# Decoder of two post-LN layers on one core: other orders of the stages on all queues, other banks for most fills, waits of the start-up at their first use

## The reference

```
x = norm(x + L0_attn(x))        # 16 heads; q, k, v lifted to a latent of 32; rotary embedding on
                                # q and k; causal softmax; latent back to 16; output projection
x = norm(x + L0_xattn(ctx, x))  # linear attention: q @ (k^T v), k and v from ctx, no softmax
x = norm(x + L0_ffn(x))         # fp4(x) @ fp4(w_gate), fp4(w_up), 704 wide; silu(g)*u; fp4; w_down
x = norm(x + L1_attn(x))        # causal softmax attention with v = x, plus a moving-average part:
                                #   e = x[1:] - y[:-1];  qa = -leaky(-q*s);  ka = sigmoid(k2*s*0.02)
                                #   y_ma = tril(qa @ ka^T) @ e
x = norm(x + L1_xattn(x, ctx, mask))  # softmax attention over ctx, output projection
x = norm(x + relu(x @ W1 + b1) @ W2 + b2)      # 1024 wide
x = norm(x + fp6(x) @ fp6(w) + b)              # one quantized linear layer
```

## Time and profile before

| | us |
|---|---|
| median of 3 runs | 916.19 (915.95 to 919.12) |
| profiled execution | 917.46 |
| its span, from first to last instruction | 915.5 |
| PE busy | 832.2 (91%) |
| PE weight loads | 667.2 (73%) |
| DVE busy | 709.4 (77%) |
| ACT busy | 635.8 (69%) |
| POOL busy | 301.5 (33%) |
| mean granted clock of TensorE | 0.968 |

### The profile page before, as it was taken

The page is one execution under the profiler, slowest core; times in us unless marked ns, Lnnn a source line. Parts: engine busy times, 40 slices in busy tenths (PEclk is TensorE's granted clock), DMA queues, the critical chain, the costliest instruction groups (busy, mean ns, idle before and its releaser), DMA issues.

```text
span 915.5 us, 29466 instructions
## 1 busy us (share of the span) xinstructions
PE 832.2 (91%) x11901; PEld 667.2 (73%) x11910; DVE 709.4 (77%) x1619; ACT 635.8 (69%) x2507; POOL 301.5 (33%) x554
## 2 busy tenths in 40 slices
PE   5877799999999999999999999999999999998873
PEld 4655677878778787878787787878787876876752
DVE  6996686878787978888787879788787878777552
ACT  3525578696959687786969686877869686866641
POOL 1232213233332434342333334342423334323221
PEclk9888799999999999999999999999999999999977
DMA  9300300000101000000001000000001000000000
GB/s 336 145 1 12 99 19 8 3 25 2 34 2 31 8 27 6 13 20 8 28 1 34 9 28 9 23 15 8 20 8 29 10 7 14 7 3 10 10 2 11
DMA packets 24440, 24.87 MB, mean 27 GB/s; under 512 B 2304, under 2 KB 22640, under 8 KB 24176
## 3 DMA queue, kind: packets, MB, share of 16 engines
q1 hardware_dynamic: 24304, 22.98, 7.7%
HBM read 18.80 MB, written 2.10 MB: 23 GB/s over the span
## 4 chain that ended last, share of the span: by engine, by line
PE 69%; ACT 17%; DVE 8%; POOL 2%; issue 2%; DMA 1%; SPq 0%; DVEq 0%; POOLq 0%; ACTq 0%
PE bank L1416 39%; PE s_tile L1416 21%; ACT prob L897 9%; PE bank L1537 3%; PE bank L1627 3%; ACT k_ L930 2%; ACT probT L836 1%; POOL rstd L762 1%; ACT x_ L945 1%; DVE stats L1127 1%; DVE y_ L1142 1%; ACT cross_ L921 1%; PE bank L1657 1%; DVE rope_ L1181 1%; ACT q_ L973 1%
## 5 line engine op out<-in xcount | busy, mean ns | idle before, releaser
L897 ACT ACTIVATE prob<-s_tile,low 128x128 f32<-128x128 f32 x768 | 273.4, 405 | 14.2 <-DVE low L1189 14.2
L897 ACT ACTIVATION_READ_ACCUMULATOR prob<-s_tile,low 128x1 f32 x768 | 188.1, 245 | 0.0
L1189 DVE TENSOR_REDUCE low<-s_tile 128x4 f32<-128x512 f32 x192 | 121.2, 680 | 31.0 <-PE s_tile L1416 30.9
L760 POOL TENSOR_TENSOR var_eps<-mean_var,rsq 128x1 f32<-128x1 f32 x144 | 31.1, 216 | 263.3 <-DVE mean_var L1129 263.1
L836 ACT ACTIVATE probT<-bank 128x512 f32<-128x512 f32 x180 | 94.1, 618 | 26.3 <-PE bank L1627 26.3
L762 POOL TENSOR_TENSOR rstd<-var_eps,rsq 128x1 f32<-128x1 f32 x144 | 86.7, 602 | 11.3
L836 ACT ACTIVATE xt_<-bank 128x256 f32<-128x256 f32 x66 | 25.4, 385 | 90.6 <-PE bank L1537 90.3
L1627 PE MATMUL bank<-cst,prob 32*128 32x32 f32 x2880 | 62.5, 225 | 17.9 <-ACT prob L897 14.9
L1627 PEld LDWEIGHTS bank<-cst,prob 32*128 32x128 f32 x2880 | 54.6, 139 | 31.1 <-ACT prob L897 18.1
L799 POOL TENSOR_TENSOR k_<-q_,q_scale 128x256 f32<-128x256 f32 x32 | 19.8, 618 | 164.4 <-DVE q_ L1088 164.4
L1416 PE MATMUL bank<-w_gu,xt_ 128*128 128x352 f32 x232 | 71.8, 460 | 0.7 <-ACT xt_ L836 0.7
(11 more groups left out here) (263 smaller groups left out, 1983.0 us busy)
## 6 DMA issues: line engine op xcount, KB each, us to landing
xtin<-in_xT SPq DMA_DIRECT2D x16, 128.0 KB, 2.4
next_<-in_x SPq DMA_DIRECT2D x16, 128.0 KB, 6.8
ct_<-in_ctxT SPq DMA_DIRECT2D x16, 128.0 KB, 7.5
w<-in_w SPq DMA_DIRECT2D x2, 1024.0 KB, 10.7
out<-x_ SPq DMA_DIRECT2D x16, 128.0 KB, 1.7
next_<-x_ SPq DMA_DIRECT2D x16, 127.0 KB
rowt<-in_rows SPq DMA_DIRECT2D x1, 1664.0 KB, 9.0
w<-in_gate_up SPq DMA_DIRECT2D x2, 512.0 KB, 6.0
```

Of the source, the lines that this page charges most:

```text
L760: pool.tensor_tensor(var_eps[:, b:b + 1], mean_var[:, b, 1:2], rsq[:, 0:1], ALU.add) .then_inc(eps_in, 1)
L897: ins = act.activation(prob[:, r, c * P:(c + 1) * P], bank[r][:, c * P:(c + 1) * P], ACT.Exp, bias=low[:, b, at0:at0 + 1], accum_out=sums[ ...
L1189: dve.tensor_reduce(low[:, b, 4 * r:4 * r + 4], rows4(src[:, :]), AX_X, ALU.max, negate=True)\
```

## The change

It changes the three tables, and moves the two blocks of waits to the stages that need them first. No stage is added or removed, and no stage's own instructions change.

*Orders.* Of PE's 918 steps 310 keep their place, the others move by 1.8 places on average, 45 at most. DVE's 736 move by 2.9 on average, nearly all of it in `x1_mask`, which goes 64 to 75 places earlier; ACT's 709 by 1.6 (241 stay, 24 at most), POOL's 304 by 1.3, SP's 73 by 3.0 (11 at most). The moves differ from tile to tile. Places before and after:

| engine, step (tile) | before | after |
|---|---|---|
| PE `l0_project` (0), `v_bias` | 3, 2 | 0, 1 |
| PE `l0_lat` (0), `l0_v` (0), `l0_v` (1) | 5, 6, 15 | 2, 3, 4 |
| PE `warm2`, `warm0`, `turn_up0` | 0, 1, 4 | 9, 22, 7 |
| PE `turn_up1`, `turn_up2` | 20, 21 | 23, 29 |
| PE `l0_scores` (0), `x0_kv` (2), `l0_project` (3) | 10, 35, 63 | 8, 43, 83 |
| PE `warm5`, `warm11`, `warm4`, `warm6` | 782, 813, 832, 901 | 775, 841, 877, 882 |
| PE `l0_mix0` (15), `l0_spread` (15) | 803, 814 | 784, 807 |
| DVE `l0_rope` (0), `quant_up1`, `quant_up2` | 5, 4, 7 | 4, 6, 13 |
| ACT `l0_norm` (8), `l1_project` (7), `l1_ka` (7) | 333, 334, 335 | 335, 333, 334 |
| SP `l0_project` (6) | 22 | 28 |

The banks of nearly all fills outside `s_tile` change, and where one bank served tiles 5 to 13 before, it now differs from tile to tile; the masks of `COVERED` follow (1,326 bits before, 1,368 after). The diff cut to lines of each kind:

```diff
-    "l0_mix0.t0": '4455644444444446', "l0_mix0.t1": '6567455555555554', "l0_mix0.t2": '3324766666666665',
+    "l0_mix0.t0": '7656567267312553', "l0_mix0.t1": '4507441054225640', "l0_mix0.t2": '6775312622677161',
...
-    "l1_project.qk2": '5712222222222227', "l1_project.k": '7030000000000051', "p_warm2": 4,
+    "l1_project.k": '3632231424320023', "l1_project.qk2": '4521016031743366', "p_warm2": 5,
...
-    ("f0_up", "f0_turn_x.xt"): 0x0002, ("f0_up", "free.s0"): 0xbff2, ("f0_up", "free.s1"): 0x7fff,
...
+    ("f0_up", "free.s0"): 0x6842, ("f0_up", "free.s1"): 0xe055, ("f0_up2", "f0_turn_x.xt"): 0xffff,
...
-            act.wait_ge(came["cols"], 16)
-            act.wait_ge(set_up, SETUP_STEPS.index("x1q_mb1") + 1)
-            act.wait_ge(cleared, 4)
+            def made(i, b, name):
+
+                if i + b == 0:
+                    act.wait_ge(set_up, SETUP_STEPS.index(name) + 1)
...
             def l1_project(i, b):
+                made(i, b, "l1k_mb1")
                 keys = wait_full(act, i, ("l1_project", b, "k"))
...
-            for n in ("wqk", "bconst"):
-                pe.wait_ge(came[n], 16)
-            pe.wait_ge(came_below, 64)
-            pe.wait_ge(part_set, 1)
-            wait_empty(pe, None, "p_v")
-            pe.wait_ge(cleared, 4)
-            pe.wait_ge(lat_set, 12)
...
             def l0_project(i, b):
                 need("l0_project", i, b, "came_xT", came_xT[b % 2], came_by(i, b // 2 + 1, 2))
                 xin = xtin[:, b % 2, :, :]
+                if i + b == 0:
+                    wait_empty(pe, None, "p_qk1")
```

More of the change, by code:

```diff
@@ L70 @@
 ORDER_AT = dict(
[L71 to L104, removed]
-        143, 199, 255, 311, 367, 423, 479, 535, 591, 647, 703, 759, 816, 870, 889), x1_scores=(86, 135, 191, 247, 303,
-        359, 415, 471, 527, 583, 639, 695, 751, 807, 860, 899), x1_mix0=(92, 148, 204, 260, 316, 372, 428, 484, 540,
-        596, 652, 708, 764, 821, 867, 902), x1_mix2=(93, 150, 205, 261, 317, 373, 429, 485, 541, 597, 653, 709, 765,
-        822, 869, 903), x1_mix1=(94, 149, 206, 262, 318, 374, 430, 486, 542, 598, 654, 710, 766, 823, 868, 904),
-        x1_mix3=(95, 151, 207, 263, 319, 375, 431, 487, 543, 599, 655, 711, 767, 824, 872, 905), x1_spread=(97, 154,
-        209, 265, 321, 377, 433, 489, 545, 601, 657, 713, 769, 828, 871, 906), x1_value=(103, 155, 211, 267, 323, 379,
-        435, 491, 547, 603, 659, 715, 771, 829, 878, 907), x1_out=(105, 157, 213, 269, 325, 381, 437, 493, 549, 605,
-        661, 717, 773, 831, 881, 908), x1_turn_h=(115, 167, 224, 281, 336, 393, 449, 505, 561, 616, 673, 729, 785,
-        842, 892, 911), x1_up=(117, 172, 229, 286, 341, 398, 454, 510, 566, 621, 678, 734, 790, 849, 894, 912),
-        x1_up2=(127, 183, 238, 294, 350, 406, 462, 518, 574, 630, 686, 742, 799, 851, 895, 913), x1_down=(129, 185,
-        240, 296, 352, 408, 464, 520, 576, 632, 688, 744, 800, 859, 898, 914), x1_down2=(130, 186, 242, 298, 354, 410,
-        466, 522, 578, 634, 690, 746, 802, 861, 900, 915), f1_turn_x=(160, 216, 272, 328, 384, 440, 496, 552, 608,
-        664, 720, 776, 837, 875, 909, 916), f1_out=(169, 223, 278, 335, 391, 447, 503, 559, 615, 670, 726, 783, 843,
-        877, 910, 917), warm5=782, warm11=813, warm9=827, warm4=832, warm8=833, warm13=835, warm3=836, warm12=857,
-        warm7=862, warm10=880, warm6=901),
@@ L881, in values, with f @@
             def values(stage):
[L882 removed]
+                def f(i, b):
+                    if i + b == 0:
+                        act.wait_ge(cleared, 1)
+                    copy(i, (stage, b, "v"), packed(v_[:, b, :, :]), lambda t: paired(t[:, 0:D]))
+                return f
             def l0_latent(i, b):
+                made(i, b, "q_bias")
                 src = wait_full(act, i, ("l0_latent", b, "q"))
```

347 lines of the change are left out of this document (207 added, 140 removed), and 44 rows, old and new, of the table BANKS.

## The result

The changed kernel takes 952.45 us (median of 4 runs, 950.62 to 953.44) beside 917.38 us for the kernel before (4 runs): a ratio of 1.0379, 95% interval 1.0351 to 1.0408. It is 35 us slower where 12 us faster was forecast, and outside the range of 898 to 918. The profiled execution took 953.44 us, with a span of 951.5.

A forecast was written before the change was run, and what follows sets the result against it. PE bounds the middle, except a stretch of about 15 us a tile where ACT does. Middle -6, head -4, tail -0.7 sum to -10.7 us: 906.8 for the profiled execution, 905.5 for the median; range 898 to 918.

The forecast's parts named there:

- SP and POOL: Queues of SP and POOL: later loads of x, earlier mask loads and moved POOL steps cost 0.
- No arithmetic is added or removed: Middle: every stage keeps its instructions; only queue orders, banks and left-out waits change.
- The middle, -6 us: Tiles between head and tail: seven tiles win 0.7 us, four win 0.3 on average; bounds -13 and +3.
- The 0.4 us a tile from PE's order: Middle, seven tiles: more PE work between `l1_turn_x` and `l1_mix3` fills the gap before the last `l1_mix`.
- The head, -4 us: First some 120 us: five items on reordered early stages and waits sum to -4 us, bounds -7 and +1.
- Item (1): Head: tile 0's `l0_project`, `v_bias`, `l0_lat` go ahead of warm stages; exponentials 4 to 5 us earlier, net -1.4 us.
- Item (3): Head: `l0_project` of tile 3 moves 20 places back to full clock, 2.03 us instead of 3.07: -1.1 us.
- Waits fewer: 0: PE's waits in the tiles' stages: 44 fewer, worth 0 to -0.4 us, taken as 0.
- The tail, -0.7: From `l0_mix` of tile 15: one warm stage of 0.65 us leaves, so -0.7 us; bounds -2 and +2.
- B: Tiles 5, 7, 9: shorter PE work uses up margins for exponentials; 1 us in every tile gives 916 us; chance 0.10.
- C: Middle: `l0` exponentials come 2 us late in nine tiles, held by a stage on ACT or DVE; 923.5 us; chance 0.08.
- D: Middle: new banks make TensorE's clock swing to half, one 5 us lapse a tile; 931 us; chance 0.02.

The follow-up runs named there:

- before_norm_late: The kernel before with only ACT's `l0_norm` of the next tile moved behind `l1_ka` in tiles 3 to 14: 913.2 us, ratio 0.9942.
- rest_new: Kernel before up to 152 PE steps, then the changed order and banks with the four stores put back; no waits left out: 931.2 us, ratio 1.0142.
- before_allwaits: The kernel before with an empty table of left-out waits, some 1,300 more waits on PE: 920.28 us, ratio 1.0023.

## Why the prediction was wrong

1. *The step that failed* is "SP and POOL": "SP's loads ... Cost 0". It followed the loads of x and of the mask through SP's new order, each with its margin, but not the stores. The store of tile t is what frees the buffer that `l0_norm` of tile t + 4 writes, and the new order puts `l1_turn_x` of tile t + 3 ahead of it in four tiles. That cost 22 of 35 us. What it needed was in sight: the wait for `stored` in ACT's norm and the two lists of places. And it priced a late transfer at 1 us at a time; measured are 2.5 to 3.7 us of wait for each, and 1.7 to 3.4 us more at half clock. With the stores put back the kernel is still 12 us slower than before, where 12 us faster was forecast; points 2 to 4 are the terms that failed besides.
2. *"No arithmetic is added or removed", with no term for PE's busy time.* Short by 8 to 9 us. The time from one stage to the next changes with what waits in it and, as it seems, with what follows.
3. *The middle, -6 us.* On ACT the size was right: 14.6 us forecast and 14.6 measured in `before_norm_late`, with a gain of 0.33 us a tile; where it arises, in ACT's wait for `x0_turn_x`, the prediction didn't say. The 0.4 us a tile from PE's order were never measured by themselves. In the changed kernel both are buried: with the stores put back the stretch from `l1_scores` of tile 3 to that of tile 14 is 13.7 us longer, where the whole middle was to be 6 shorter. One reading was wrong: the queries' bank is outside 0 to 3 in tile 11 too (bank 4). The forecast signs came out split: PE's waits on `l1_ka` fell from 9.5 us to 3.8 as said (2.7 of it is one of the four stalls), those on the exponentials to 1.7 (6 to 12 was said), since there is no longer one place where PE waits for them.
4. *The head, -4 us.* Item (1) had the exponentials of tile 0 at 28 us, and they start at 27.85; but the gain ends where the prediction itself placed DVE's weights, and nothing of it is left there, not the 1.4 us counted. Item (3) was right: `l0_project` of tile 3 now stands at full clock and takes 1.95 us, not 3.07. All the same the changed head lost some 3 us, half of it by tile 3.
5. *Waits fewer: 0.* Right.
6. *The tail, -0.7.* `l1_scores` of tile 14 is 14.0 us late with the stores put back and the end 12.0: -2, in its bounds; part of it is the warm stages that moved ahead.
7. *The rivals.* B is nearest to what remains besides the seams, margins of a few tenths used up elsewhere, with a price of 10.7 us and a chance of 0.10: after the stores are put back the kernel is 12 us slower than before. C, the slower case, named a slip in the wrong queue. D did not come: between 125 and 870 us the clock of the changed kernel leaves 1.00 only at its four pauses of 2.2 to 2.9 us, and with the stores put back nowhere. So the rule of the Trainium skill, TensorE: Matmul & The Clock Gate, section "A second HAM failure mode: psum-queue depth-cycling", is not borne out by these banks. One spell is unlike the others: in `rest_new` 3.4 us at half clock begin at 134.7 us, behind a pause of 1.49 us, while the same pause of 1.38 and 1.48 us in the kernel before and in `before_allwaits` left the clock at 1.00.

The range failed for want of one case: that something in a queue which has hardly any work is late by more than its margin in some tiles. The tile-by-tile differences of the new order made that more likely, since each of 16 tiles had to be followed by itself.
